# A first block turned and multiplied in halves, its root taken from the variance, and one weight split moved to GpSimd

## The reference

```python
xn = (x - mean(x)) / sqrt(var(x) + 1e-5)
# attention: y = xn @ U (128 x 32); dist_sq[t, j] = |y_t - y_j|^2 within a block
attn = softmax(-dist_sq) @ xn
# experts: shared one of width 1024, and 8 routed ones of width 512, two for each token
xr = xn * rsqrt(mean(xn * xn) + eps)          # for the router alone
probs = softmax(xr @ router_w.T); top 2, weights normalised, capacity 320 tokens for each expert
shared = (silu(xn @ sg) * (xn @ su)) @ sd
routed = scatter_add over experts of w * ((silu(xg @ rg) * (xg @ ru)) @ rd)
out = x + attn + shared + routed
```

## Time and profile before

| | us |
|---|---|
| median of 3 runs (lowest, highest) | 156.56 (156.55, 156.57) |
| profiled execution | 156.54 |
| its span (first to last instruction) | 155.0 |
| busy: PE, DVE, ACT, POOL | 149.7, 122.4, 109.5, 86.6 |

### The profile page before, as it was taken

One profiled execution on the slowest core, in us unless ns is written; L12 is line 12 of the kernel. 1 busy time (PEld: TensorE's weight loads), 2 busy tenths in 40 slices (PEclk: granted clock), 3 DMA queues, 4 the chain that ended last, 5 costly groups with the idle time before them and its releaser, 6 DMA issues.

```text
span 155.0 us, 3095 instructions
## 1 busy us (share of the span) xinstructions
PE 149.7 (97%) x928; PEld 132.9 (86%) x928; DVE 122.4 (79%) x299; ACT 109.5 (71%) x227; POOL 86.6 (56%) x111
## 2 busy tenths in 40 slices
PE   6899999999999999999999999999999999999991
PEld 6878777889998888898888999999999998788791
DVE  3999969999827999877998677867867865778973
ACT  3369999999595987657865687896775663644850
POOL 7653432767777788777653063689877374460000
PEclk9999999999999999999999999999999999999999
DMA  4999999981110076451259307112221010193572
GB/s 127 299 272 122 189 300 349 339 269 56 52 52 6 9 233 200 132 147 40 68 121 294 141 2 207 39 41 74 84 77 30 28 36 25 31 289 97 196 203 68
DMA packets 26638, 20.72 MB, mean 134 GB/s; under 512 B 2335, under 2 KB 22837, under 8 KB 26624
## 3 DMA queue, kind: packets, MB, share of 16 engines
q1 hardware_dynamic: 24544, 17.76, 42.9%
q0 software_dynamic: 1792, 2.65, 5.4%
q10 hardware_dynamic: 288, 0.14, 0.3%
HBM read 12.36 MB, written 7.92 MB: 131 GB/s over the span
## 4 chain that ended last, share of the span: by engine, by line
PE 84%; DVE 8%; DMA 2%; ACT 1%; issue 1%; POOL 1%; DVEq 0%
PE bank L1242 8%; PE bank L1244 8%; PE bank L1243 8%; PE bank L1371 7%; PE bank L1368 7%; PE bank L1365 7%; PE bank L1327 7%; PE bank L1466 7%; PE bank L1467 7%; PE bank L1468 7%; PE bank L1484 3%; PE bank L1312 2%; DMA acc<-in_L_attn_x_dram 2%; PE bank L1495 2%; PE bank L1340 1%
## 5 line engine op out<-in xcount | busy, mean ns | idle before, releaser
L716 ACT ACTIVATE silu<-bank 128x512 f32<-128x512 f32 (+1 forms) x64 | 33.2, 519 | 27.6 <-PE bank L1371 27.2
L1063 DVE TENSOR_TENSOR bank<-bank,silu 128x320 f32<-128x320 f32 (+1 forms) x56 | 32.7, 584 | 18.8 <-ACT silu L716 12.1
L606 POOL DMA_INDIRECT slots_dram<-row,slot_i x32 | 34.9, 1092 | 10.3 <-issue 9.5
L625 POOL DMA_INDIRECT routed_dram<-eo,xg x24 | 23.3, 970 | 15.8 <-DVE eo L1103 10.6
L1069 DVE TENSOR_TENSOR hid_lo<-bank,hid_hi 128x320 fp32r<-128x320 f32 (+1 forms) x56 | 31.7, 565 | 0.0
L724 ACT CAST hid_hi<-bank 128x320 fp32r<-128x320 f32 (+1 forms) x56 | 27.5, 492 | 0.4 <-DVE bank L1063 0.4
L1365 PE MATMUL bank<-xnT_hi,sw_hi 128*128 128x512 f32 x31 | 13.0, 418 | 0.0
L613 POOL TENSOR_TENSOR ew_lo<-sw_raw,ew_hi 128x1024 fp32r<-128x1024 f32 x3 | 7.2, 2396 | 9.8 <-ACT ew_hi L740 9.8
L1371 PE MATMUL bank<-xnT_hi,sw_lo 128*128 128x512 f32 x31 | 12.3, 397 | 0.0
L1242 PE MATMUL bank<-xnT_hi,sw_hi 128*128 128x512 f32 x31 | 12.3, 397 | 0.0
L1368 PE MATMUL bank<-xnT_lo,sw_hi 128*128 128x512 f32 x31 | 12.3, 396 | 0.0
(11 more groups left out here) (228 smaller groups left out, 387.5 us busy)
## 6 DMA issues: line engine op xcount, KB each, us to landing
sw_raw<-in_L_ffn_rg_dram SPq DMA_DIRECT2D x8, 256.0 KB, 3.2
sw_raw<-in_L_ffn_ru_dram SPq DMA_DIRECT2D x8, 256.0 KB, 3.2
rd_raw<-in_L_ffn_rd_dram SPq DMA_DIRECT2D x8, 256.0 KB, 3.8
routed_dram<-fill SPq DMA_DIRECT2D x1, 2048.0 KB, 12.2
routed<-routed_dram SPq DMA_DIRECT2D x8, 256.0 KB, 3.9
slots_dram<-fill SPq DMA_DIRECT2D x1, 1300.0 KB, 12.3
xg<-slots_dram SPq DMA_DIRECT2D x8, 130.0 KB, 2.7
row<-row SPq DMA_DIRECT2D x1, 1024.0 KB, 7.8
```

Of the source, the lines that this page charges most:

```text
L606: G.indirect_dma_start(slots_dram, bass.IndirectOffsetOnAxis(slot_i[:, k, t:t + 1], 0), row[:, t, 0:RW], None, bounds_check=E * CAP - 1, o ...
L625: G.indirect_dma_start(routed_dram, bass.IndirectOffsetOnAxis(xg[0:n, e % XB, r, 1:2].bitcast(I32), 0), eo[0:n, e % 2, r, :], None, bounds ...
L716: C.activation(silu[:, q % 2, 0:n], gate_bank(q)[:, 0:n], ACT.Silu).then_inc(silu_ready, 1)
L1063: V.tensor_tensor(hid, up[:, 0:n], silu[:, q % 2, 0:n], ALU.mult).then_inc(hid_ready, 1)
```

## The change

Block 0 and what feeds it are done in another way:

- DVE normalises three of block 0's tiles, POOL none; POOL takes the third split of the shared weights, which DVE gives up.
- ACT takes block 0's root from the aggregated variance itself, with the scale and the eps as a bias; DVE's `ve` is then needed by the reciprocal only, and its row 1 is computed for all blocks at once in the second pass. In the second pass ACT takes two roots, one for each row.
- ACT rounds the first quarter of the shared weights ahead of its tile.
- PE turns block 0 in two halves of two tiles into two banks; ACT and DVE round and split each half by itself; and chunk 0 is multiplied in two halves of 256 columns.
- The projections do both products on the high part of the tokens first and wait for the remainder only before the third.
- Chunks 2 to 5 of block 0 wait for the rounded weights at their start and for the remainder before the gate's third product.
- 40 warming matmuls instead of 60, then 15 ahead of the turning, none after it.

```diff
-    ON_DVE = [2, 3, 2, 2]
-    ON_POOL = [1, 0, 1, 1]
+    ON_DVE = [3, 3, 2, 2]
+    ON_POOL = [0, 0, 1, 1]
...  # SP, ahead of the first experts' weights
-            sp.wait_ge(sw_ready, CS // 2 - 1)
-            sp.wait_ge(sw_ready_dve, 1)
+            sp.wait_ge(sw_ready, CS // 2)
...  # POOL
-            normalize(0)
             split_shared(0)
             split_shared(1)
+            split_shared(2)
...
-            pool.wait_ge(sw_ready_dve, 1)
             normalize(2)
...  # ACT
             def root_of(gs):
                 ts = slice(TG * gs[0], TG * (gs[-1] + 1))
-                act.wait_ge(ve_ready, pass_of[gs[0]] + 1)
-                C.activation(root[:, :, ts], ve[:, :, ts], ACT.Sqrt, scale=0.25).then_inc(root_ready, 1)
+                act.wait_ge(mv_ready, pass_of[gs[0]] + 1)
+                last = C.activation(root[:, 0, ts], mv[:, ts, 1], ACT.Sqrt, scale=0.25, bias=quarter_eps[:, 0:1])
+                if gs is PASSES[-1]:
+                    last = C.activation(root[:, 1, :], mv[:, :, 1], ACT.Sqrt, scale=0.25 * (1.0 + RMS_EPS),
+                                        bias=quarter_eps[:, 1:2])
+                last.then_inc(root_ready, 1)
+            def first_turned_hi(h):
+                cols = slice(2 * P * h, 2 * P * (h + 1))
+                act.wait_ge(first_turned, h + 1)
+                C.copy(xnT_hi[:, cols], first_tokens_b[h][:, 0:2 * P]).then_inc(xnT_hi_s, 1)
...
+            act.wait_ge(eps_set, 1)
             root_of(PASSES[0])
+            round_shared(0)
             normalize(0)
-            round_shared(0)
-            turned_hi(0)
+            first_turned_hi(0)
+            first_turned_hi(1)
             round_shared(1)
...
             act.wait_ge(rw_turned, 1)
+            act.wait_ge(xnT_ready, 1)
             C.copy(rw_hi, rw_ps).then_inc(rw_hi_s, 1)
...  # DVE
             def variances_of(gs):
...
-                then(last)
-                V.tensor_scalar(ve[:, 0, ts], mv[:, ts, 1], LN_EPS, None, ALU.add)
-                V.tensor_scalar(ve[:, 1, ts], mv[:, ts, 1], 1.0 + RMS_EPS, LN_EPS * RMS_EPS, ALU.mult, ALU.add
-                                ).then_inc(ve_ready, 1)
-                dve.wait_ge(ve_ready, pass_of[gs[0]] + 1)
-                mark(V.reciprocal(nw_a[:, :, ts], ve[:, :, ts]))
+                last.then_inc(mv_ready, 1)
+                dve.wait_ge(mv_ready, pass_of[gs[0]] + 1)
+                last = V.tensor_scalar(ve[:, 0, ts], mv[:, ts, 1], LN_EPS, None, ALU.add)
+                if gs is PASSES[-1]:
+                    last = V.tensor_scalar(ve[:, 1, :], mv[:, :, 1], 1.0 + RMS_EPS, LN_EPS * RMS_EPS, ALU.mult, ALU.add)
+                then(last)
+                fs = flat_of(gs)
+                mark(V.reciprocal(nw_a[:, fs], ve_flat[:, fs]))
...
+            def first_turned_lo(h):
+                cols = slice(2 * P * h, 2 * P * (h + 1))
+                dve.wait_ge(xnT_hi_s, h + 1)
+                V.tensor_tensor(xnT_lo[:, cols], first_tokens_b[h][:, 0:2 * P], xnT_hi[:, cols].bitcast(F32),
+                                ALU.subtract).then_inc((first_lo, xnT_ready)[h], 1)
...
             normalize(0)
             stats_of(1)
+            first_turned_lo(0)
+            first_turned_lo(1)
             stats_of(2)
-            turned_lo(0)
             stats_of(3)
...
             mult_chunk(0)
-            third = slice(4 * P, 6 * P)
-            dve.wait_ge(sw_hi_s, 3)
-            V.tensor_tensor(sw_lo[:, :, third], sw_raw[:, :, third], sw_hi[:, :, third].bitcast(F32), ALU.subtract
-                            ).then_inc(sw_ready_dve, 1)
             normalize(2)
...  # PE
+            def turn_first():
+                for h in range(2):
+                    if h == 0:
+                        pe.wait_ge(first_pair, 1)       # DVE's second tile
+                    else:
+                        pe.wait_ge(xn_ready, 1)
+                        pe.wait_ge(xn_ready_act, 1)
+                    for j in range(2 * h, 2 * h + 2):
+                        last = nc.tensor.transpose(first_tokens_b[h][:, P * (j % 2):P * (j % 2) + P], xn[:, j, :],
+                                                   ident[:, :])
+                    last.then_inc(first_turned, 1)
...  # first_chunk: the six matmuls for each half of 256 columns, with waits for its high part, sw_ready and its low part
...
-            warm(WARMING)
+            warm(2 * WARMING // 3)
...
-            turn(0)
-            warm(10)
+            warm(WARMING // 4)
+            turn_first()
             first_chunk()
```

More of the change, by code:

```diff
@@ L170, in moe_attention_kernel @@
         root = sb("root", [P, 2, NT])
-        nw_a = sb("nw_a", [P, 2, NT])
-        nw_b = sb("nw_b", [P, 2, NT])
-        nw_c = sb("nw_c", [P, 2, NT])
+        nw_a = sb("nw_a", [P, 2 * NT])
+        nw_b = sb("nw_b", [P, 2 * NT])
+        nw_c = sb("nw_c", [P, 2 * NT])
         rstd = sb("rstd", [P, 2, NT])
+        quarter_eps = sb("quarter_eps", [P, 2])
+        ve_flat, root_flat, rstd_flat = [t[:, :, :].rearrange("p k t -> p (k t)") for t in (ve, root, rstd)]
         nmr = sb("nmr", [P, NT])
@@ L276, in out_turn_bank @@
             return end_turn_b if job == len(JOBS) - 1 else turn_b[1]
-        tokens_b = [bank[6], bank[0], bank[3], bank[0]]
+        first_tokens_b = [bank[6], bank[7]]
+        tokens_b = [None, bank[0], bank[3], bank[0]]
         y_b = [bank[4], bank[6], bank[5], bank[7]]
@@ L332, in moe_attention_kernel @@
         dve_step = sem("dve_step")
-        ve_ready = sem("ve_ready")
+        eps_set, mv_ready = sem("eps_set"), sem("mv_ready")
         root_ready = sem("root_ready")
+        first_pair, first_turned, first_lo = sem("first_pair"), sem("first_turned"), sem("first_lo")
         rstd_ready, nmr_ready = sem("rstd_ready"), sem("nmr_ready")
@@ L356, in moe_attention_kernel @@
         att_done, att_added = sem("att_done"), sem("att_added")
-        sw_hi_s, sw_ready, sw_ready_dve = sem("sw_hi_s"), sem("sw_ready"), sem("sw_ready_dve")
+        sw_hi_s, sw_ready = sem("sw_hi_s"), sem("sw_ready")
         ew_hi_s, ew_split_dve, ew_split_pool = sem("ew_hi_s"), sem("ew_split_dve"), sem("ew_split_pool")
@@ L883, in then @@
                 settle()
+            V.memset(quarter_eps[:, 0:1], 0.25 * LN_EPS)
+            V.memset(quarter_eps[:, 1:2], 0.25 * LN_EPS * RMS_EPS).then_inc(eps_set, 1)
             V.memset(fill[:, 0:1], 0.0)
@@ L906, in stats_of, with flat_of @@
                 mark(last)
+            def flat_of(gs):
+                return slice(0, TG) if gs is PASSES[0] else slice(TG, 2 * NT)
             def variances_of(gs):
@@ L929, in rstd_of @@
                 settle()
[L930 to L933, removed]
+                fs = flat_of(gs)
+                then(V.tensor_tensor(nw_b[:, fs], nw_a[:, fs], root_flat[:, fs], ALU.mult))
+                then(V.scalar_tensor_tensor(out=nw_c[:, fs], in0=nw_b[:, fs], scalar=-4.0,
+                                            in1=root_flat[:, fs], op0=ALU.mult, op1=ALU.mult))
+                V.scalar_tensor_tensor(out=rstd_flat[:, fs], in0=nw_c[:, fs], scalar=3.0, in1=nw_b[:, fs],
                                        op0=ALU.add, op1=ALU.mult).then_inc(rstd_ready, 1)
@@ L943, in normalize @@
                                            ALU.subtract, ALU.mult)
+                    if t == 1:
+                        last.then_inc(first_pair, 1)
                 last.then_inc(xn_ready, 1)
@@ L1276, in project @@
                 cols = slice(S * g, S * g + S)
-                pe.wait_ge(xnT_ready, g + 1)
+                pe.wait_ge(xnT_hi_s, g + 2)
                 if g == 0:
@@ L1283, in project @@
                     pe.wait_ge(hid_ready, g + 1)
-                parts(y_b[g][0:3 * R + E, :], UW_hi[:, :], UW_lo[:, :], xnT_hi[:, cols], xnT_lo[:, cols]
-                      ).then_inc(y_done, 1)
+                y = y_b[g][0:3 * R + E, :]
+                M(y, UW_hi[:, :], xnT_hi[:, cols], start=True, stop=False)
+                M(y, UW_lo[:, :], xnT_hi[:, cols], start=False, stop=False)
+                pe.wait_ge(xnT_ready, g + 1)
+                M(y, UW_hi[:, :], xnT_lo[:, cols], start=False, stop=True).then_inc(y_done, 1)
             def norms():
@@ L1396, in first_chunk @@
                 w_hi, w_lo = sw_hi[:, :, 0:P], sw_lo[:, :, 0:P]
-                m_hi, m_lo = xnT_hi[:, 0:S], xnT_lo[:, 0:S]
-                gate, up = gate_bank(0)[:, :], up_bank(0)[:, :]
                 pe.wait_ge(sw_hi_s, 1)
[L1400 to L1408, removed]
+                for h in range(2):
+                    cols = slice(2 * P * h, 2 * P * (h + 1))
+                    m_hi, m_lo = xnT_hi[:, cols], xnT_lo[:, cols]
+                    gate, up = gate_bank(0)[:, cols], up_bank(0)[:, cols]
+                    pe.wait_ge(xnT_hi_s, h + 1)
+                    M(gate, w_hi[:, 0, :], m_hi, start=True, stop=False)
+                    M(up, w_hi[:, 1, :], m_hi, start=True, stop=False)
+                    pe.wait_ge(sw_ready, 1)
```

(11 more changed lines are left out.)

4 lines of the change are left out of this document (2 added, 2 removed).

## The result

The changed kernel takes 158.56 us, the median of six runs (157.49 to 158.65); the kernel before took 156.56 (156.44 to 156.77) beside it. The ratio is 1.0103, with a 95% interval of 1.0083 to 1.0124: 2.0 us slower, where 0.2 were forecast, and outside the range. Four of the six runs stood at 158.52 to 158.65 with a mean granted clock of about 0.988, two at 157.49 and 157.58 with 1.000, so the median is that of runs in which TensorE's clock fell for a while. The profiled execution is one of the four: 158.65, span 156.9.

The account below looks back on a forecast made before the run. The prediction took PE's chain up to 21.57 us to bound the kernel, then a slackless DVE queue, then PE. +0.34 - 0.12 = +0.22 on 156.54 gave 156.76, set at 156.77 against the median; range 155.85 to 157.1.

Parts of the forecast that it names:

- Pass 1, DVE: First normalising pass: ACT's root runs beside DVE's held add, so DVE's tiles start 0.10 us earlier (bounds 0 and 0.35).
- at nothing: List of edits priced at zero, among them DVE's two memsets before its wait for x.
- Rival 3: POOL's first split starts before nmr, delaying nmr and all first-block tiles: +0.5, 157.05 us; chance 0.12.
- Rival 4: Less warming and longer PE idling lower the clock for the first two chunks: 1.5 to 3 us more; chance 0.05.
- A: Post-measurement theory, not forecast: the activation-table load slipped behind ACT's wait ahead of the first root.
- B: Post-measurement theory, not forecast: DVE was late enough for POOL's split to get in ahead of nmr.
- The hold by POOL's split: First block: POOL's split holds DVE's normalising tiles, so tile 1 ends at 7.6 (bounds 6.70 and 7.75).
- nine tiles: Evidence weighed against the hold: normalising tiles averaged 343 ns, including two beside POOL's own tile.
- Block 1's transposes: Pass 2: PE's transposes of block 1 start at 14.66 instead of 14.32, +0.34 us.
- The last projection: High-part products first, so no wait for the last remainder: the gap of 0.35 becomes 0.235, -0.12 us.
- The shift through the routing: Whatever moves before the logits' transposes at 21.57 moves the end equally; the DVE stretch after has no slack.
- The prediction's sum: +0.34 for block 1's transposes, -0.12 for the last projection: +0.22 us, giving 156.77; chance 0.45.

Follow-up runs that it names:

- e2: The kernel before with one more wait, for a long-set semaphore, ahead of ACT's first root: 157.83 us, ratio 1.0081.
- the execution at the high clock: A single execution of the unaltered changed kernel, run for a profile at the high clock: 157.79 us.
- e4: The changed kernel with POOL's first split waiting until DVE has done its three tiles, table load still late: 156.74 us, ratio 1.0003.
- e1: The changed kernel without ACT's wait for the eps constants ahead of the first root: 156.75 us, ratio 1.0005.
- e5: The changed kernel with one wait ahead of the first root and POOL's first split after DVE's three tiles: 156.31 us, ratio 0.9976.
- after_look2: A second single execution of the unaltered changed kernel, run for a profile; its clock was low for longer: 159.88 us.

## Why the prediction was wrong

**The step that failed** is in "Pass 1, DVE": "after the change the root runs beside the held add", taken as 0.10 earlier, with bounds of 0 and 0.35. ACT needs its table load ahead of that root. In the kernel before, the root had a single wait, and the load ran at 1.96, in ACT's idle time (e2, which adds nothing but a wait, shows that the waits alone decide this). The change put a second wait ahead of it, and the load came to stand behind the wait that ends last. So the root was 1.40 later than forecast (6.21 for 4.81, where the held add begins) and 1.00 later than before. The prediction priced the memsets of the new constant "at nothing" and did not ask what the wait for them does to the instructions behind it in ACT's queue; ACT's idle time before the root was never looked into. The Trainium skill (ScalarE: Activation LUTs, "Step-by-step: what each stage is for") says that the load is placed right before the activation that needs it; all profiles here agree, whichever side of a wait it falls on. Under "What ACT_TABLE_LOAD costs" the page gives 2.66 us for a load with its drain; here the load takes 1.28 and the root follows 0.02 after it, so 1.28 is the price, and no drain shows.

**Rival 3 happened, by another door.** "The split starts before nmr", priced at +0.5, was to decide "from a landing before about 5.35". The weights did not land early; DVE came late. Nor was it a toss-up: ACT's rounding, for which the split waits, now stands right behind the late root, and so does DVE's Newton step. In the result the split starts 0.89 after the root and nmr 0.92 after it, and the other three profiles of the changed kernel repeat both within 0.01. Everything behind stood until the split ended. What it cost on top of the late load is the execution at the high clock against e4: 157.79 - 157.0 = 0.8 (one profile each; x's statistics begin at 3.34 and 3.59 in them, so counted from there it is 1.0).

**Rival 4 happened too**, with 0.05 as its chance: PE idled from 6.80 to 8.95 and the clock fell. Its place was right (the first two chunks), its price 0.9 in one profile and 2.1 in another for "1.5 to 3". (The lower level that it read from the earlier trace rows is read from the distance of the matmuls; the granted clock of both rows is 1.00.) It was taken as independent of the others. It is not: A and B together make the idle time long; in e1, e2, e4 and e5, where one or both are missing, no run has a mean clock under 0.997. How long it gets then hangs on the pace of the warming.

The 2.1 between the profiled executions (156.54 and 158.65) come apart along e5, e4, the execution at the high clock and the result: -0.2 for the change without A and B (156.33), +0.7 for the late load (157.0), +0.8 for the split ahead of nmr (157.79), +0.9 for the clock. Counted from the start of x's statistics (3.49, 3.39, 3.59, 3.34 and 3.54 in the five) they are -0.1, +0.5, +1.0 and +0.7; that is an estimate, for not all of the first pass follows x. In medians the first two steps are -0.3 and +0.4, and then come the high-clock runs of 157.44 to 157.98 and the low ones from 158.5 on. The order of the steps matters: with the load early, the split's own hold costs 156.75 - 156.31 = 0.4 (e1 and e5). And the late load, 1.3 in the kernel before (e2), is only 0.4 between e5 and e4, for e5 loses much of its head start at the hold in the second pass: its aggregates are done 1.0 earlier than e4's (root at 11.05 for 12.07), the product nw_b behind the hold only 0.3 (12.49 for 12.79).

**What held.** The hold by POOL's split, weighed against nine tiles that showed nothing: 1.30 in e1, 1.25 in the result, 0.89 in e5. The Trainium skill (SBUF — State Buffer, "Who interferes with whom") names both kinds, a tensor_scalar in a two-port mode and an operation with two SBUF inputs. nmr is of the second kind; the tile of e1 is a tensor_scalar, and in which mode it ran no trace here shows. The nine tiles were no evidence against it for a split: the two at 6.20 ran beside POOL's own tile, another operation. Why that one let DVE's second tile through, and a split does not, stays open. Block 1's transposes, forecast 0.34 late: in e1 they come 14.42 - 3.27 = 11.15 after x's statistics begin, before 14.32 - 3.49 = 10.83: 0.32 late. The last projection: 0.23, to the hundredth. The shift through the routing: 2.30 at the y split. The prediction's sum was thus sound for a kernel that differs from this one by a single wait: +0.22 forecast, +0.17 between the medians of e1 and the kernel before beside it (156.75 and 156.58).

## What to carry to other kernels

When an edit gives an activation a second wait, look where its table load stands in the trace of before: a load that lies in idle time is free only as long as nothing that ends late stands ahead of it. Write such a constant where an existing wait covers it; here the wait for the variance did, since DVE writes both, one after the other. And when two engines start within a few hundredths of each other on a resource that one of them keeps, price both orders, for a delay elsewhere picks the order. Delays that meet on one engine aren't independent: they add up to one idle time, and that one has to be priced for the clock.

## What the runs showed of the hardware

- A load of the activation table takes 1.28 in every profile, wherever it stands.
- An operation of four elements for each partition on DVE took 1.25 where a split of 512 on POOL had begun 0.03 to 0.04 ahead of it, in all four profiles of the changed kernel, at either clock; it took 0.16 in e4, where the split came later.
- The low level of the granted clock (1.2 GHz) lasted past the return of work: the stretch from 8.8 to 12.2 has 0.51 in the result's profile, with PE back at work from 8.95, and in after_look2 the stretch from 12.2 to 16.0 still has 0.62, a mean of both levels, with PE busy throughout.
- The root with a bias read from memory takes 0.30, the one without 0.21 (e1 and the kernel before).
